# One AdaLN transformer block: all eight PSUM banks in one pool with the softmax normalisation moved to transfers, and the four-bit quantising with its grid constant from two bit operations

## The reference, cut to what matters

```python
h = _layernorm(x) * (1 + ca) + sa
x = x + ga * attn(h, ...)          # scores + slope * (k - q), causal, softmax, times V, out @ o_w.T + o_b
h = _layernorm(x) * (1 + cb) + sb
x = x + gb * ffn(h, ...)

def fp4_quant_dequant(x):          # blocks of 16 along the last axis
    scale = maximum(max(abs(xb)) / 6.0, 1e-12)
    xn = xb / scale
    idx = searchsorted([0.25, 0.75, 1.25, 1.75, 2.5, 3.5, 5.0], abs(xn))
    return [0, 0.5, 1, 1.5, 2, 3, 4, 6][idx] * sign(xn) * scale

h = silu(fp4_linear(x, w_gate)) * fp4_linear(x, w_up)
return fp4_linear(h, w_down)       # fp4_linear quantises both operands
```

## Time and profile before

| | |
|---|---|
| median of 3 runs | 4182.7 us (4179.85 to 4183.4) |
| the profiled execution | 4182.51 us, its span 4180.7 us |
| TensorE busy | 3731.8 us, 89% of the span |
| VectorE, ScalarE, POOL busy | 3130.8, 1946.8 and 1196.2 us |
| granted TensorE clock, mean | 0.967 |

### The profile page before, as it was taken

How to read it: one execution, slowest core, us unless ns; L and a number is a source line. 1 busy time by engine, 2 the same in 40 slices (tenths; PEclk the granted TensorE clock), 3 DMA queues, 4 the chain that set the end, 5 groups by cost and what they waited for, 6 DMA issues and landing times.

```text
span 4180.7 us, 58634 instructions
## 1 busy us (share of the span) xinstructions
PE 3731.8 (89%) x22068; PEld 1974.5 (47%) x22068; DVE 3130.8 (75%) x6125; ACT 1946.8 (47%) x3535; POOL 1196.2 (29%) x886
## 2 busy tenths in 40 slices
PE   1799999999989989999999999999999998999886
PEld 0334454454545445454544545445454544544445
DVE  7477768778786787877777786777877688776855
ACT  2255444544444554444444454454544455445441
POOL 2222314132231323223132331423224132321223
PEclk6799999999999999999999999999999999999997
DMA  2532122213122122212213122222212212212000
GB/s 76 71 57 33 39 43 45 40 34 51 30 48 45 28 46 41 49 34 46 43 29 52 34 44 46 37 41 37 51 31 52 46 25 49 41 27 45 11 15 10
DMA packets 127981, 169.89 MB, mean 41 GB/s; under 512 B 22020, under 2 KB 75988, under 8 KB 127700
## 3 DMA queue, kind: packets, MB, share of 16 engines
q1 hardware_dynamic: 127700, 166.15, 22.8%
HBM read 47.01 MB, written 16.84 MB: 15 GB/s over the span
## 4 chain that ended last, share of the span: by engine, by line
PE 73%; DVE 13%; ACT 9%; issue 2%; SPq 1%; DMA 1%; POOL 1%; DVEq 0%; ACTq 0%; POOLq 0%
PE o_acc L635 13%; PE banks L655 10%; PE banks L619 9%; PE banks L753 8%; PE banks L730 7%; PE banks L737 7%; ACT arena L815 7%; PE banks L686 4%; PE banks L711 3%; PE banks L694 3%; PE banks L746 2%; DVE banks L1020 2%; DVE tm L993 2%; PE banks L622 1%; PE banks L671 1%
## 5 line engine op out<-in xcount | busy, mean ns | idle before, releaser
L815 ACT ACTIVATE arena<-banks 128x512 f32<-128x512 f32 (+1 forms) x2432 | 1289.4, 576 | 1239.7 <-PE banks L622 702.9
L1020 DVE CUSTOM_DVE_ANT_0 banks<-banks,mask 128x640 f32<-128x640 f32 (+3 forms) x1024 | 1038.0, 1040 | 228.1 <-PE banks L655 218.3
L619 PE MATMUL banks<-qa,ka 105*128 105x512 bf16 (+3 forms) x3072 | 852.3, 332 | 154.3 <-ACT arena L815 125.4
L655 PE MATMUL banks<-ka,qa 102*128 102x512 bf16 (+3 forms) x3072 | 761.6, 334 | 104.7 <-DVE top L1020 80.1
L635 PE MATMUL o_acc<-arena,va 128*17 128x512 f32 (+3 forms) x6144 | 642.4, 500 | 13.1 <-ACT arena L815 12.5
L619 PEld LDWEIGHTS banks<-qa,ka 105*128 105x128 bf16 x3072 | 280.2, 98 | 674.1 <-ACT arena L815 471.2
L655 PEld LDWEIGHTS banks<-ka,qa 102*128 102x128 bf16 x3072 | 267.1, 99 | 484.8 <-DVE top L1020 150.9
L1018 DVE TENSOR_REDUCE top<-banks 128x2 f32<-128x768 f32 (+3 forms) x384 | 391.6, 1043 | 138.5 <-PE banks L660 107.8
L937 POOL TENSOR_TENSOR hid<-hid,tm 128x704 f32<-128x704 f32 x128 | 214.7, 1678 | 900.1 <-DVE hid L994 900.1
L753 PE MATMUL banks<-wdT,hqT 128*128 128x256 f32 x1536 | 371.2, 393 | 3.6 <-ACT hqT L846 3.2
L730 PE MATMUL banks<-wguT,xqT 128*128 128x352 f32 x1024 | 337.0, 463 | 2.8 <-ACT hqT L846 2.0
(11 more groups left out here) (148 smaller groups left out, 4929.5 us busy)
## 6 DMA issues: line engine op xcount, KB each, us to landing
qa<-parts SPq DMA_DIRECT2D x384, 128.0 KB, 4.6
ka<-parts SPq DMA_DIRECT2D x384, 128.0 KB, 6.2
xa<-in_x SPq DMA_DIRECT2D x16, 1024.0 KB, 5.2
xr<-in_x SPq DMA_DIRECT2D x64, 256.0 KB, 2.8
out_x<-xr SPq DMA_DIRECT2D x64, 256.0 KB, 2.1
ffn_rows<-rows_dram SPq DMA_DIRECT2D x16, 384.0 KB, 4.2
ga_row<-rows_dram SPq DMA_DIRECT2D x16, 128.0 KB, 2.9
qa<-in_w_mod SPq DMA_DIRECT2D x2, 768.0 KB, 5.6
```

The source lines that it names most:

```text
L619: mm = pe.matmul(ps[:, m * w:(m + 1) * w], ka[g][0:KT, h, kt * P:(kt + 1) * P], qa[g][0:KT, h, q0:q0 + w], start=heads < G, stop=heads == ...
L655: mm = pe.matmul(ps[:, at:at + z - a], qa[g][0:KS, h0 + m, qt * P:(qt + 1) * P], ka[g][0:KS, h0 + m, a:z], start=qt > 0, stop=qt == 0 or h ...
L815: nc.scalar.activation(probs[:, s % P_SLOTS, j * heads:(j + 1) * heads, 0:w], ps[:, 0:heads * w].rearrange("p (h q) -> p h q", h=heads), A ...
L1020: nc.vector.tensor_tensor_reduce(out=ps, in0=ps, in1=mask[:, S - w:S], scale=1.0, scalar=MASKED, op0=ALU.add, op1=ALU.max, accum_out=tops) ...
```

## The change

Five things change together.

1. All eight banks are one pool. `o_acc` is gone: PV takes a bank of the pool at the first piece of each half and holds it until ScalarE's copy of that half. STEPS now runs through all of half 0 (four pieces) and then all of half 1 (eight), so the two halves of a group are open one after the other. CO is two jobs, one a half. Ring D may be 3 ahead.
2. ON and OT are gone, with their TensorE transposes (eight a group and sixteen a batch), the reciprocal and product on VectorE and the copies on ScalarE. In their place, for each group, SP issues DEN (the sums of `oT`, laid over 128 partitions in `sums`), NUM (four transfers of the heads' rows from `oT` to `onT`), RDW (reciprocals from SBUF to DRAM) and RBC (from DRAM to 64 partitions of `rsumT`, each head's row repeated 16 times). VectorE takes the reciprocal of 128 by 32 sums (RD), and POOL multiplies `onT` by `rsumT` (MUL), once for two groups. O reads `onT`.
3. Quantising: the power of two of each element and its grid constant come from one instruction with an `and` and an `or`; a maximum with MAGIC is folded into the addition. VectorE has three full passes in place of four, POOL three in place of two. The scale is kept negative so that the order of the subtraction can turn round.
4. The due time of S moves from 20 to 30 before its place, and some costs in the plan are changed.
5. VectorE clears all eight banks at the start; SM uses four instructions of one kind.

```diff
-STEPS = [(kt, c) for kt in range(T) for c in range(2) if c == 1 or kt < T // 2]
+STEPS = [(kt, c) for c in range(2) for kt in range((c + 1) * T // 2)]
+FIRST, LAST = (0, T // 2), (T // 2 - 1, NS - 1)
...
-    BANKS, AHEAD = 6, {"A": 4, "D": 2, "Q": 2}
+    BANKS, AHEAD = 8, {"A": 4, "D": 3, "Q": 2}
...
-                due = at + L * n / (NG * sum(h * (q + 1) * P for q, _, h in TILES)) - 20.0
+                due = at + L * n / (NG * sum(h * (q + 1) * P for q, _, h in TILES)) - 30.0
...
+                      banks=1 if s in FIRST else 0, holder=("ACT", ("CO", b, g, c)) if s in FIRST else None)
+                if s in LAST:
+                    past = (b, g - 1) if g else (b - 1, NG - 1)
+                    p.add("ACT", ("CO", b, g, c), 0.6, due, ("PE", ("PV", b, g, s)), ("SP", ("NUM", *past)), ("SP", ("DEN", *past)))
+            normalise(b, g, due)
+
+    def normalise(b, g, due):
+
+        old = (b, g - 1) if g else (b - 1, NG - 1)
+        done = [("ACT", ("CO", b, g, c)) for c in range(2)]
+        p.add("SP", ("DEN", b, g), 0.7, due, *done, ("DVE", ("RD", *old)), lag=2.5)
+        p.add("SP", ("NUM", b, g), 2.6, due + 1, *done, ("PE", ("O", b - 1, NPAIR - 1)), lag=3.0)
+        p.add("DVE", ("RD", b, g), 0.4, due, ("SP", ("DEN", b, g)), ("SP", ("RDW", *old)))
+        p.add("SP", ("RDW", b, g), 0.7, due, ("DVE", ("RD", b, g)), ("SP", ("RBC", *old)), lag=2.5)
+        p.add("SP", ("RBC", b, g), 0.7, due, ("SP", ("RDW", b, g)), ("POOL", ("MUL", b, g // 2 - 1) if g >= 2 else ("MUL", b - 1, C - 1)), lag=3.0)
+        if g % 2:
+            p.add("POOL", ("MUL", b, g // 2), 2.2, due + 10.0, *((("SP", (k, b, n)) for n in (g - 1, g) for k in ("NUM", "RBC"))))
...
-            pe(("O", b, r), 1.75, at + 2.0 + r, ("ACT", ("OT", b, 0, r // 2)), ("ACT", ("OT", b, 1, r // 2)), ("POOL", ("WG", b)),
+            pe(("O", b, r), 1.75, at + 2.0 + r, ("POOL", ("MUL", b, 0)), ("POOL", ("MUL", b, 1)), ("POOL", ("WG", b)),
...
+                        sp.dma_start(sums[:, :], oT[HD:P:P // G, :]).then_inc(sums_in, 16)
+                        for h in range(G):
+                            sp.dma_start(onT[half + HD * h:half + HD * (h + 1), g // 2, :],
+                                         oT[P // G * h:P // G * h + HD, :]).then_inc(outputs_in, 16)
+                    sp.dma_start(rsum_dram[g].rearrange("h (p q) -> (h p) q", q=G * S // P), rsums[:, :]).then_inc(rsums_out, 16)
+                    sp.dma_start(rsumT[half:half + 64, :], rsum_dram[g].unsqueeze(1).broadcast_to((G, HD, S))).then_inc(rsumT_in, 16)
...
-                        nc.gpsimd.tensor_tensor(u, u, m, ALU.subtract).then_inc(gridded, 1)
-                        pool.wait_ge(gridded, done)
+                        nc.gpsimd.tensor_scalar(m, m, MAGIC, 1.0, ALU.max, ALU.mult).then_inc(gridded, 1)
+                        pool.wait_ge(gridded, 2 * done - 1)
+                        nc.gpsimd.tensor_tensor(u, m, u, ALU.subtract).then_inc(gridded, 1)
+                        pool.wait_ge(gridded, 2 * done)
+                    elif kind == "MUL":
+                        c = e[2]
+                        n = b * NG + 2 * c + 2
+                        pool.wait_ge(outputs_in, 64 * n)
+                        pool.wait_ge(rsumT_in, 16 * n)
+                        nc.gpsimd.tensor_tensor(onT[:, c, :], onT[:, c, :], rsumT[:, :], ALU.mult).then_inc(normal, 1)
...
-                step(nc.vector.scalar_tensor_tensor(out=blocks(u), in0=blocks(u), scalar=BELOW, in1=spread(iv),
+                step(nc.vector.scalar_tensor_tensor(out=blocks(u), in0=blocks(u), scalar=-BELOW, in1=spread(iv),
                                                     op0=ALU.mult, op1=ALU.mult))
-                step(nc.vector.tensor_scalar(m.bitcast(U32), u.bitcast(U32), 0x7F800000, None, ALU.bitwise_and))
-                step(nc.vector.tensor_scalar(m, m, 1.0, MAGIC, ALU.max, ALU.mult))
-                return nc.vector.tensor_tensor(u, u, m, ALU.add)
+                step(nc.vector.tensor_scalar(m.bitcast(U32), u.bitcast(U32), 0x40800000, 0x0B400000, ALU.bitwise_and, ALU.bitwise_or))
+                return nc.vector.scalar_tensor_tensor(out=u, in0=m, scalar=MAGIC, in1=u, op0=ALU.max, op1=ALU.add)
```

More of the change, by code:

```diff
@@ L84, with add @@
     RINGS = {"A": ("PE", "ACT"), "D": ("PE", "DVE"), "Q": ("DVE", "POOL")}
-    BANKS, AHEAD = 6, {"A": 4, "D": 2, "Q": 2}
+    BANKS, AHEAD = 8, {"A": 4, "D": 3, "Q": 2}
     def __init__(self):
         self.jobs, self.order = {}, {e: [] for e in ("PE", "ACT", "DVE", "POOL", "SP")}
-        self.bank, self.before = {}, {}
-    def add(self, engine, event, cost, due, *after, lag=0.06, ring=None, takes=None, lock=None, banks=0):
+        self.bank, self.before, self.holder = {}, {}, {}
+    def add(self, engine, event, cost, due, *after, lag=0.06, ring=None, takes=None, lock=None, banks=0, holder=None):
         self.jobs[engine, event] = (cost, due, [a for a in after if a], lag, ring, takes, lock, banks)
+        if banks:
+            self.holder[event] = holder or (self.RINGS[ring][1], event)
     def settle(self):
@@ L554, in open_banks @@
                         pe.wait_ge(sem, done)
+                copied = [(o[1] * NG + o[2]) * 2 + o[3] + 1 for o in PLAN.before[e] if o and o[0] == "CO"]
+                if copied:
+                    pe.wait_ge(o_free, max(copied))
                 return bank(e)
@@ L561, in setup @@
                         ps = open_setup(e)
+                        pe.wait_ge(banks_clear, 1)
                         pe.wait_ge(ident_set, 4)
```

161 lines of the change are left out of this document (84 added, 77 removed).

## The result

| | before | changed |
|---|---|---|
| median | 4181.27 us | 4320.35 us (4 runs, 4315.65 to 4331.8) |
| ratio | | 1.034, 95% interval 1.031 to 1.036 |
| the profiled execution | 4182.51 us | 4331.8 us, its span 4329.7 |
| granted TensorE clock, mean | 0.967 | 0.936 |

The change makes the kernel 3.4% slower; I had forecast 4.5% faster, with a range that ended at 4130.

The account below looks back on a forecast made before the run. TensorE, busy 92% in the steady part, was taken as the bound, idling mostly in T's and S's waits for banks. Terms -91 - 120 - 10 + 30 + 4 = -187 took 4182.5 to 3996 us, range 3860 to 4130.

Parts of the forecast that it names:

- Transposes, -91: TensorE's ON and OT transposes: removing 5.7 us a batch, hidden by nothing, saves 91 us over 16 batches.
- Banks, -120: T and S waiting for banks: the larger pool saves 0 to 198 us, taken at 60%, 120 us.
- VectorE, -10: VectorE's dropped quantising pass and ON product: 11.8 us a batch less work, felt only by S's waits, saving 10 us.
- POOL, "hidden": POOL's added quantising pass and MUL: 13.2 us a batch more, hidden by attention jobs beside each feed-forward.
- Transfers, +30: Transfer chain behind a group's last PV: 14.1 to 18.8 us, so the projection waits 2 us a batch, +30.
- (d): Rival: the projection waits for the transfers; slower from 14.5 us a batch, 4266 us at 20; chance 0.07.
- The ends, +4: Start and tail: last batch's chain adds 3.3 us and the tail's quantising 0.5; clearing banks 0; +4 for both.
- T's weight loads below 250: Sign on TensorE: the waits of T's weight loads for ScalarE fall from 455 us to under 250.
- Projection wait 0 to 3 us: Sign at the projection's first matmul: a wait for POOL of 0 to 3 us a batch.
- Period 237: Sign in the long middle part: the period between projections falls from 248.9 to about 237 us.
- Clock at 0.99: Sign on TensorE: the granted clock stays at 0.99 in the steady part.
- the three signs of error: Projection wait over 5 us a batch; T's waits above 350 us; a new wait for POOL's quantised tiles before HT or XT.

Follow-up runs that it names:

- the fastest kernel: Changed kernel with the old quantising, RBC in four pieces, and at each batch's last group the MOVE issued behind RBC: 4003.83 us, ratio 0.957.
- the banks alone: Changed kernel's pool of eight banks, order by halves, ring D at 3 and due time 30, but ON, OT and quantising of before: 4043.99 us, ratio 0.967.
- The kernel without the chain: Banks and transfers with the old quantising, but without DEN, the reciprocal, RDW, RBC and MUL; output not normalised: 3870.3 us, ratio 0.926.

## Why the prediction was wrong, step by step

**Transposes, -91.** Nothing speaks against it, but no run takes them away alone. TensorE's busy time is 80 us less in the fastest kernel than with the banks alone (3603.2 against 3682.8). There is also a wait that I had not given them, as I read only TensorE's own time at the earlier trace rows: with the banks alone S waits 45.2 us for VectorE's product of ON (L1064 above). The kernel without the chain is 174 us below the banks alone, but it leaves out the whole normalisation.

**Banks, -120.** Measured -138, so the size was near, and that was luck: the mechanism was not what I said. I gave T's waits for ScalarE most of the gain, 65% of 259 us, and with the banks alone T's weight loads still wait 370.5 us of the 455.0 in the earlier trace rows. 86 of the 138 us come with S being allowed ahead, where I had 30 in all (0.29 x 103). With the old ring and due time these waits are shorter, 279.9 us, yet the kernel is 86 us slower. The count over its placement, taken as in the prediction, is 71 T jobs of 2432, where the faster kernel has 763. The count told how often a bank was close behind, and not which wait ends last.

**VectorE, -10.** Not measured: where POOL's pass is quick the difference is within the spread of the runs. The busy time fell 94.5 us, though, not 190. Most of what is missing is SM, whose new instructions (item 5 of the change) had no term in my sum: the four groups were busy 55.4 us and now are 128.9. One of them, before and after:

```profile
L1028 DVE TENSOR_TENSOR top_parts<-top_rest,top_parts 128x32 bf16<-128x32 f32 x64 | 13.1, 205 | 2.2
```

```profile
L1079 DVE SCALAR_TENSOR_TENSOR top_parts<-top_rest,top_parts 128x32 bf16<-128x32 f32 x64 | 37.7, 589 | 2.2
```

Again it is POOL beside them: of the 256 instructions of SM, 12 had a POOL instruction beside them before and 155 have one after; the others take at most 0.19 us in both kernels. The layer norm's pass adds 20 us, and the addition with the maximum in it 11.

**POOL, "hidden".** This step failed, and it cost the most. I priced the pass by the nearest one-tensor row, 1157 ns for 1024 columns, without asking whether the operation matters. It does: 0.78 us with products, 2.56 with a maximum. I took the one row as both ends of a cost that the trace didn't show, and no rival had a dearer one. 1.8 us more on a tile then aren't hidden, since HT waits for POOL with a short lead: its waits for POOL in the stretch are 120.2 us with the maximum and 16.7 without. The operation costs 181 us, the whole new quantising 171, and on the kernel before 114. The part beyond HT's waits isn't taken apart: TensorE is busy 57 us longer with the maximum (3689.3 against 3632.5), and the rest is other idle time.

**Transfers, +30.** This step failed too. In the kernel with banks and transfers alone the wait is 125.1 us in the long stretch, 8.3 a batch where I had 2, and making it nearly vanish was worth 145 us. Three terms of the chain show in the trace. RBC was off: 6.4 us to MUL (7.3 in the changed kernel) where I took 2.9 from ga_row, of one outer dimension; its four source rows put it on a quarter of the engines. RDW was not: I had "at worst 6.2" and at the place shown it was 4.8. The end of the queue before it was missing: SP was still issuing the query's MOVE, for 2.2 us after the copy. And I had no term for the clock behind the wait, some 33 us in the projection.

**The rivals.** (d) is the mechanism that came about, but with 8 to 9 us a batch, not 20: I let each us of wait count once in each batch, 15 us in all; it cost 1.15 times as much, some 18 us for 16 batches. Against it stood 179 us, by which the fastest kernel, with almost no such wait, is below the one before. By that the wait decides from about 10 us a batch (179 / 18), an estimate, where I had 14.5. At 8.3 the kernel with banks and transfers alone is still 0.8% faster. The slower sign comes from POOL's maximum, which was no rival of mine, only a line among what would show me wrong.

**The ends, +4.** From the last copy's end to the projection it was 16.7 us (4162.95 to 4179.60), where I had 9.7. RBC again: 8.3 us to MUL, with two transfers behind it, where I had 2.9.

**What I named to show it.** T's weight loads below 250 (238.6, right). Projection wait 0 to 3 us (8.7). Period 237 (258.0). VectorE -190 (-94.5), POOL +210 (+534.5). Clock at 0.99 (0.96). Of the three signs of error, the two that came were the right ones.

## What to carry to other kernels

Ask of a chain of small transfers not what each takes, but what stands ahead of each in its issuing queue and on how many transfer engines its shape puts it: two such edits, with the arithmetic unchanged, took 145 us from 4149. Price an operation on POOL by a row with the same operation: here one of the same shape was three times off. Give a stall of TensorE its wait and the matmuls at the lower clock behind it, here 1.15 times the wait; and take its price from kernels that keep TensorE's order, since the kernel without the chain made it look like twice. Ask of every VectorE pass with two tensors in SBUF what POOL does beside it.

## What the runs showed of the hardware

- POOL's pass with a maximum over 704 f32 columns took 2.56 us, with two products 0.78; the maximum alone over 512 columns 1.50, two products 0.62.
- A transfer of 256 KB from four source rows to 64 partitions had 0.19 to 0.27 of the 16 transfer engines busy at 70 to 82 GB/s and was done after 6.4 us (7.3 with two more transfers issued behind it); in four pieces 0.55, 131 GB/s and 3.7 us.
- A transfer of 16 KB took 1.4 to 2.8 us with no MOVE ahead of it and 3.9 to 6.4 behind one, six transfers of 128 KB.
- In 8.8 us in which TensorE had nothing to do its granted clock fell to 0.50. It was still 0.50 in the first 5 us of the projection and 1.00 behind: 32 matmuls took 9.8 us in place of 7.14.
- A VectorE pass with two tensors in SBUF (128x256) took at most 0.49 us with no POOL instruction beside it, and 1.85 us in the mean of the 56 that had one, of which 55 ended 0.27 to 0.29 us after the POOL instruction's end. VectorE's product of a tensor in SBUF with one in PSUM (L1165, 128x704) took 0.88 to 0.89 us in the mean with POOL beside it or not.
